# Decoder block on one core: batch 2's state ahead of the experts' first product, products on ones in TensorE's waits, and the last tile in four groups

## The reference

```python
x = _layernorm(x + ssm(x))                  # 32 complex states, linear recurrence over the 256 tokens
x = _layernorm(x + int8_expert(x, w, dw))   # per batch: smooth-quant linear, silu(gate) * up, smooth-quant linear
x = _layernorm(x + moe(x))                  # 8 experts of width 176, top 2 of 8, all experts computed densely
...
def moe(h):
    combine = top-2 softmax shares of h @ router_w.T
    for e in range(8):
        gate, up = split(h @ gate_up[e].T)
        out += combine[:, e] * ((silu(gate) * up) @ down[e].T)
```

## Time and profile before

| | |
|---|---|
| median of 3 runs | 182.44 us (182.42 to 182.51) |
| profiled execution, its own time | 181.19 us |
| its span, first to last instruction | 179.4 us |
| busy: PE, DVE, ACT, POOL | 153.3, 122.2, 88.9, 51.0 us |
| mean granted TensorE clock | 0.931 of full speed |

### The profile page before, as it was taken

The page is one execution under the profiler, slowest core; times in us unless marked ns, Lnnn a source line. Parts: engine busy times, 40 slices in busy tenths (PEclk is TensorE's granted clock), DMA queues, the critical chain, the costliest instruction groups (busy, mean ns, idle before and its releaser), DMA issues. The chain is left out here.

```text
span 179.4 us, 3021 instructions
## 1 busy us (share of the span) xinstructions
PE 153.3 (85%) x1020; PEld 141.9 (79%) x1020; DVE 122.2 (68%) x439; ACT 88.9 (50%) x211; POOL 51.0 (28%) x107
## 2 busy tenths in 40 slices
PE   7971294574969989999999999999999999999990
PEld 7850272343859979899999789999999998999980
DVE  4886777767479849668886787489567467453632
ACT  7301878663534187683224878544565523253330
POOL 5713994867901031300016211001223002100011
PEclk9999579555599999999999999999999999999999
DMA  4999930000000000000000000000000000000000
GB/s 123 290 391 394 352 120 5 0 0 0 0 2 0 5 0 0 0 4 0 0 0 33 2 27 2 4 0 0 31 4 29 0 2 4 29 29 4 0 29 29
DMA packets 6463, 8.72 MB, mean 49 GB/s; under 512 B 560, under 2 KB 6192, under 8 KB 6192
## 3 DMA queue, kind: packets, MB, share of 16 engines
q1 hardware_dynamic: 6448, 8.53, 13.8%
HBM read 7.48 MB, written 1.05 MB: 48 GB/s over the span
## 5 line engine op out<-in xcount | busy, mean ns | idle before, releaser
L284 PE MATMUL ps_gu<-gu_hi,x_hi 128*128 128x352 f32 (+1 forms) x128 | 44.7, 350 | 1.6 <-DVE hid L1487 1.6
L285 PE MATMUL ps_gu<-gu_lo,x_hi 128*128 128x352 f32 (+1 forms) x128 | 41.7, 326 | 0.0
L1487 DVE SCALAR_TENSOR_TENSOR hid<-sil,combine,ps_gu 128x176 f32<-128x176 f32 x64 | 24.1, 390 | 17.3 <-ACT sil L712 16.8
L712 ACT ACTIVATE sil<-ps_gu 128x176 f32<-128x176 f32 x64 | 19.7, 318 | 32.1 <-PE ps_gu L289 31.8
L289 PE MATMUL ps_gu<-gu_hi,x_lo 128*128 128x352 f32 (+1 forms) x128 | 31.5, 327 | 0.0
L284 PEld LDWEIGHTS ps_gu<-gu_hi,x_hi 128*128 128x128 f32 x128 | 24.5, 191 | 2.2 <-issue 1.9
L264 PE MATMUL ps_out<-dp_hi,hid_hi 128*128 128x256 f32 x88 | 25.1, 285 | 0.0
L285 PEld LDWEIGHTS ps_gu<-gu_lo,x_hi 128*128 128x128 f32 x128 | 24.5, 191 | 0.1
L265 PE MATMUL ps_out<-dp_lo,hid_hi 128*128 128x256 f32 x88 | 24.4, 278 | 0.0
L266 PE MATMUL ps_out<-dp_hi,hid_lo 128*128 128x256 f32 x88 | 24.4, 277 | 0.0
L289 PEld LDWEIGHTS ps_gu<-gu_hi,x_lo 128*128 128x128 f32 x128 | 22.5, 190 | 0.5 <-DVE x_lo L1440 0.5
(11 more groups left out here) (252 smaller groups left out, 289.6 us busy)
## 6 DMA issues: line engine op xcount, KB each, us to landing
gu_raw<-in_guT SPq DMA_DIRECT2D x1, 2824.0 KB, 11.6
dp_raw<-in_dpT SPq DMA_DIRECT2D x1, 1408.0 KB, 15.3
u_feat<-in_xT SPq DMA_DIRECT2D x4, 256.0 KB, 4.7
w_feat<-in_wT SPq DMA_DIRECT2D x4, 256.0 KB, 9.4
out<-u_feat SPq DMA_DIRECT2D x8, 128.0 KB, 1.7
dw_feat<-in_dwT SPq DMA_DIRECT2D x4, 128.0 KB, 7.2
c_raw<-in_c SPq DMA_DIRECT2D x2, 128.0 KB, 3.6
bt<-in_bT SPq DMA_DIRECT2D x1, 128.0 KB, 2.2
```

The source lines that it names most:

```text
L284: pe.matmul(dst, x2_hi[:, b % 2, c, tok], gu_hi[:, c, col], start=(c == 0), stop=False)
L285: pe.matmul(dst, x2_hi[:, b % 2, c, tok], gu_lo[:, c, col], start=False, stop=False)
L712: act.activation(sil[:, bank_of(b, k)], ps_gu[:, bank_of(b, k), E:E + H], ACT.Silu).then_inc(sil_ready, 1)
L1487: dve.scalar_tensor_tensor(hid[:, t, e * H:(e + 1) * H], sil[:, n], combine[:, t, e:e + 1], ps_gu[:, n, E + H:E + GU], ALU.mult, ALU.mult) ...
```

## The change

Four things change, and the calls of all engines are put in a new order around them.

1. `ps_state` of batch 2 becomes bank 0 of `ps_gu`, the bank of the first slot. `state_in(2)` comes behind `expert_in(0)`, `state_out(2, *)` and DVE's, POOL's and ACT's parts of batch 2's state also come ahead of `gate_up(0, 0)`, which now waits for `x1_ready` of batch 2. Batch 1's `state_out` and DVE's scan of batch 1 move ahead of batch 0's statistics and transposes, too.
2. `keep_busy` gets a bank as an argument and is called at 13 places with 87 products in all instead of 2 places with 18, the last one ahead of `gate_up(0, 0)`.
3. `down` is cut into `down_first`, which waits only for the high half of the group, and `down_second`, which waits for the low one. The products are the same.
4. The last tile's third group is cut into two (`LAST_GROUPS`): one chunk, then two.

```diff
+LAST_GROUPS = [(0, 4), (4, 8), (8, 9), (9, HC)]
...
-        ps_state = [ps_s[:], ps_gu[:, 0], ps_s[:], ps_s[:]]
+        ps_state = [ps_s[:], ps_gu[:, 0], ps_gu[:, 0], ps_s[:]]
...
-                    pe.wait_ge(x1_ready, halves(1))
+                    pe.wait_ge(x1_ready, halves(2))
...
+            def down_first(b, t, g):
+                lo, hi = groups(b, t)[g]
+                pe.wait_ge(hid_hi_ready, count_of(b, t, g))
...
                 for c in range(lo, hi):
-                    last = split_matmul(ps_out[:, 0:D], hid_hi[:, c], hid_lo[:, c], dp_hi[:, c], dp_lo[:, c],
-                                        c == 0, c == HC - 1)
-                if g == NG - 1:
+                    pe.matmul(ps_out[:, 0:D], hid_hi[:, c], dp_hi[:, c], start=(c == 0), stop=False)
+                    pe.matmul(ps_out[:, 0:D], hid_hi[:, c], dp_lo[:, c], start=False, stop=False)
+
+            def down_second(b, t, g):
+                lo, hi = groups(b, t)[g]
+                pe.wait_ge(hid_lo_ready, count_of(b, t, g))
+                for c in range(lo, hi):
+                    last = pe.matmul(ps_out[:, 0:D], hid_lo[:, c], dp_hi[:, c], start=False, stop=(c == HC - 1))
+                if hi == HC:
                     last.then_inc(moe_done, 1)
...
-                if b > 1:
+                if b == 2:
+
+                    pe.wait_ge(x1_ready, halves(1))
+                if b == 3:
 
                     pe.wait_ge(rows_ready, b)
...
-                if b == 1:
-
-                    pe.wait_ge(rows_ready, 1)
+                if b in (1, 2):
+
+                    pe.wait_ge(rows_ready, b)
                 transpose_blocks(ps_x[b], tokens[:, b], x1T_done)
...
-            def keep_busy(n):
+            def keep_busy(bank, n):
                 for _ in range(n):
-                    pe.matmul(ps_gu[:, 2, 0:P], ones[:], ones[:], start=True, stop=True)
+                    pe.matmul(bank[:, 0:P], ones[:], ones[:], start=True, stop=True)
...
+            keep_busy(ps_tr, 2)
             expert_in(0)
+            state_in(2)
             x1_transpose(1)
+            keep_busy(ps_tr, 15)
             as2_transpose(0)
             dws2_transpose(0)
+            keep_busy(ps_gu[:, 1], 2)
+            state_out(2, 0)
             scale2_broadcast(0)
+            dq_transpose(0)
             aq_transpose(0)
-            dq_transpose(0)
+            keep_busy(ps_gu[:, 1], 2)
             expert_out(0)
+            state_out(2, 1)
             xs_transpose(1)
             ws_transpose(1)
+            keep_busy(ps_gu[:, 1], 16)
             x2_transpose(0)
             xq_transpose(1)
+            keep_busy(ps_gu[:, 1], 5)
             gate_up(0, 0)
...
+            hid_transpose(3, 1, 3)
+            down_second(3, 1, 1)
+            down_first(3, 1, 2)
+            down_second(3, 1, 2)
+            down_first(3, 1, 3)
+            down_second(3, 1, 3)
```

More of the change, by code:

```diff
@@ L52, with groups, experts_to, count_of @@
 SLOT_OF = {te: k for k, te in enumerate(SLOT_ORDER)}
-ALL = [(t, g) for t in range(TT) for g in range(NG)]
-def count_of(b, group):
-    return b * len(ALL) + ALL.index(group) + 1
+def groups(b, t):
+    return LAST_GROUPS if (b, t) == (B - 1, TT - 1) else GROUPS
+def experts_to(chunk):
+    return -(-chunk * P // H)
+def count_of(b, t, g):
+    return (b * TT + t) * NG + g + 1
 def halves(b):
@@ L478, in _ @@
             state_out_s_first(1)
+            keep_busy(ps_gu[:, 2], 6)
+            state_out(1, 0)
             x1_transpose(0)
+            state_out(1, 1)
+            keep_busy(ps_tr, 7)
             xs_transpose(0)
@@ L504, in _ @@
             expert_in(1)
+            x1_transpose(2)
             gate_up(0, 3)
-            state_in(2)
             gate_up(0, 4)
             gate_up(0, 5)
-            gate_up(0, 6)
             hid_transpose(0, 0, 0)
             as2_transpose(1)
-            state_out(2, 0)
-            state_out(2, 1)
             dws2_transpose(1)
+            gate_up(0, 6)
             gate_up(0, 7)
@@ L517, in _ @@
             scale2_broadcast(1)
-            gate_up(0, 9)
-            hid_transpose(0, 0, 1)
             aq_transpose(1)
             dq_transpose(1)
-            x1_transpose(2)
+            gate_up(0, 9)
             expert_out(1)
@@ L525, in _ @@
             gate_up(0, 11)
-            down(0, 0, 0)
+            xs_transpose(2)
+            gate_up(0, 12)
+            hid_transpose(0, 0, 1)
             ws_transpose(2)
-            gate_up(0, 12)
-            xs_transpose(2)
+            down_first(0, 0, 0)
+            down_second(0, 0, 0)
+            hid_transpose(0, 0, 2)
             gate_up(0, 13)
             gate_up(0, 14)
-            hid_transpose(0, 0, 2)
             x2_transpose(1)
+            gate_up(0, 15)
             xq_transpose(2)
-            gate_up(0, 15)
-            down(0, 0, 1)
+            down_first(0, 0, 1)
             scale_broadcast(2)
-            wq_transpose(2)
             hid_transpose(0, 1, 0)
@@ L541, in _ @@
             gate_up(1, 1)
-            down(0, 0, 2)
+            down_second(0, 0, 1)
+            hid_transpose(0, 1, 1)
+            wq_transpose(2)
+            down_first(0, 0, 2)
+            down_second(0, 0, 2)
+            expert_in(2)
+            down_first(0, 1, 0)
             gate_up(1, 2)
-            expert_in(2)
-            hid_transpose(0, 1, 1)
-            down(0, 1, 0)
             gate_up(1, 3)
             state_in(3)
+            down_second(0, 1, 0)
+            hid_transpose(0, 1, 2)
+            down_first(0, 1, 1)
+            down_second(0, 1, 1)
             gate_up(1, 4)
-            hid_transpose(0, 1, 2)
             gate_up(1, 5)
-            down(0, 1, 1)
-            down(0, 1, 2)
             state_out(3, 0)
@@ L571, in _ @@
             gate_up(1, 12)
+            down_first(1, 0, 0)
             ws_transpose(3)
             xs_transpose(3)
+            down_second(1, 0, 0)
             gate_up(1, 13)
-            hid_transpose(1, 0, 2)
-            down(1, 0, 0)
             gate_up(1, 14)
             xq_transpose(3)
+            hid_transpose(1, 0, 2)
             x2_transpose(2)
@@ L581, in _ @@
             gate_up(1, 15)
-            down(1, 0, 1)
+            down_first(1, 0, 1)
+            down_second(1, 0, 1)
+            down_first(1, 0, 2)
             scale_broadcast(3)
@@ L585, in _ @@
             gate_up(2, 0)
+            down_second(1, 0, 2)
+            expert_in(3)
             gate_up(2, 1)
-            down(1, 0, 2)
             gate_up(2, 2)
-            expert_in(3)
+            down_first(1, 1, 0)
             hid_transpose(1, 1, 1)
-            down(1, 1, 0)
+            down_second(1, 1, 0)
             gate_up(2, 3)
@@ L594, in _ @@
             hid_transpose(1, 1, 2)
+            down_first(1, 1, 1)
+            down_second(1, 1, 1)
             gate_up(2, 5)
-            down(1, 1, 1)
             gate_up(2, 6)
@@ L599, in _ @@
             dws2_transpose(3)
-            down(1, 1, 2)
+            down_first(1, 1, 2)
             gate_up(2, 7)
+            down_second(1, 1, 2)
+            hid_transpose(2, 0, 0)
+            scale2_broadcast(3)
             gate_up(2, 8)
-            hid_transpose(2, 0, 0)
             aq_transpose(3)
@@ L859, in _ @@
             smooth_w(1)
+            x1_norm(2, 0)
+            x1_norm(2, 1)
+            quant_x(1, 0)
             x2_norm(0, 1)
-            quant_x(1, 0)
             quant_x(1, 1)
@@ L1663, in _ @@
             route_shares(2)
-            moe_add(1, 0)
-            gate_scale(3)
             hidden(2, 0)
+            hidden(2, 1)
+            expert_act(3)
+            hidden(2, 2)
             hid_lo_sub(1, 1, 1)
-            hidden(2, 1)
-            hidden(2, 2)
-            up_scale(3)
-            expert_act(3)
             act_ratio(3)
```

380 lines of the change are left out of this document (193 added, 187 removed).

## The result

| | before | after |
|---|---|---|
| median of 4 runs | 182.43 us (182.27 to 182.51) | 175.97 us (175.34 to 176.17) |
| profiled execution, its span | 181.19, 179.4 us | 176.10, 174.3 us |
| PE busy, mean granted clock | 153.3 us, 0.931 | 162.3 us, 0.999 |

The account below looks back on a forecast made before the run. The end was taken as the slots' start plus PE's work behind it, some 3 us of waits and a 4.6 us tail. 4.55 + 0.25 - 0.7 = 4.1 us off the median 182.44 gave 178.3 us, range 176.6 to 180.8.

Parts of the forecast that it names:

- the chain by hand: Batch 0's steps up to the fourth slot, followed at full clock: first slot 1.4 us late, fourth slot 0.25 us early.
- slower rival: Ahead of the first slot, products on ones run at half clock and delay the chain: 184.9 us, chance 0.07.
- I apply the difference to the median: Last step of the sum: 4.1 us, reckoned on the profiled execution of 181.19 us, taken off the median: 182.44 - 4.1 = 178.3 us.
- the 1.25 us: Amount by which the median of the kernel before stood above its profiled execution of 181.19 us.
- at most the 0.5 us: In the full stretch, cutting `down` can remove at most the 0.5 us that PE waited for `hid_lo`.
- 0.8 us of small waits ... I leave them: PE's small waits behind the first slot, 0.8 us, may go or be replaced; left out of the sum.
- 4.55 - 0.7: Full stretch: 4.55 us off for batch 2's state, transposes and their wait, less a new 0.7 us wait.
- The new wait for `as2`: `as2_transpose(1)`, behind slot 5, at 56.2 us on PE with its operand ready at 56.9: 0.7 us added.
- 0.25 were forecast: Ahead of the stretch: the fourth slot comes at 52.85 instead of 53.10 us, 0.25 us early.
- The rival in which the small waits go: Head's fillers cost less at `xs` (0.9), no new wait (0.7), small waits go (0.5): 176.2 us, chance 0.14.
- no change: PE's freed time all turns into waits behind 54 us: within 0.2% (0.36 us), chance 0.03.
- the shorter list meets DVE: Behind 54 us, batch 1's and 2's expert chains have less time, so waits of 1 to 3 us: around 180.3 us, chance 0.16.

Follow-up runs that it names:

- the head's 15: The changed kernel without the 15 products on ones behind `state_in(1)`, the other 72 kept: 175.53 us, ratio 0.9653.
- the earlier transfer: The changed kernel with the experts' weights' transfer issued ahead of batch 2's and 3's inputs: 175.74 us; also without the 15 products behind `state_in(1)`: 174.36 us.
- the execution of 183.3 us: The profiled execution of the kernel before, run again unchanged: 183.3 us; median of those 12 runs 181.93 us.
- the last five products: The changed kernel without the five products on ones directly ahead of the first slot: 176.01 us, ratio 0.9660.

## Why the prediction was right, and where it was wrong

**Right: the picture, and the chain by hand.** The end is the start of the slots, plus PE's work, plus a few waits, plus 4.6 us. `expert_in(0)` was put at 27.3 and came at 27.37, `expert_act(0)` at 30.74 and 30.96, `expert_out(0)` at 37.6 and 37.63, the first slot at 46.7 and 46.64, the second at 48.7 and 48.62, the fourth at 52.85 and 53.08. The stretch is the same within 0.2 us in all profiled executions of one order (121.6 to 121.8 before, 116.5 to 116.6 after, where the cut is in), and putting the state back costs its work and more.

That the absolute times fit so well is partly luck. `xs_transpose(0)` was put at 22.1 by the products at the head and DVE's chain behind them, and came at 22.13, but what held it was the experts' weights: they landed at 18.85 us, 1.14 later than in the execution shown before (17.71), and it stands 3.28 behind. In five other executions of the same head it came between 21.35 and 22.75. The intervals behind it are the reckoning's own merit: 5.2 us to `expert_in(0)` were forecast, 5.24 measured.

The full clock was an assumption of the chain, and what it is worth was in no term of its own: 3.6 us in the changed kernel. The slower rival rested on its failing, with a chance of 0.07; the clock held. The Trainium skill (TensorE: Matmul & The Clock Gate, Part 1) says that activity releases the throttle; the pair with and without the products agrees, 0.999 against 0.942 mean clock and 176.1 against 179.4 us. By the same page's Part 2, matmuls stay in program order, so a product on ones in no wait delays what follows: the head's 15 did, `x1_transpose(0)` by 1.68 us. No effect on the end was shown for it in the changed kernel, where the landing holds `xs` anyway; with the earlier transfer it was 1.4 us.

**Wrong, first: "I apply the difference to the median", the last step of the sum.** In the profiles the time went down by 181.19 - 176.10 = 5.09 us, in the medians by 6.46. These 1.37 us are more than half of the miss of 2.33. The execution shown before lay at the low end of its kernel's (181.03 to 183.65 us over all runs, 182.1 in the median), the one after near its median. Its mean clock of 0.931 was reached in 4 of the 103 other executions of that kernel whose clock is on record, at 181.1 to 181.4 us; 70 had 0.924 or less, and 182.3 us in the median. It also had the earliest landing of the experts' weights seen in that order, and the execution shown after a late one.

What made the execution of 183.3 us longer lies all ahead of the fourth slot: 1.09 us from weights that land later, at `xs`, and 0.92 between `xs` and the fourth slot. The 0.92 is clock, all of it: 0.63 in `state_out(1, 0)` and 0.29 in the second slot, with no new wait beside them (the copy of `down`'s weights came 1.08 us later, but so did `xs`). The changed order keeps its clock, and its DVE doesn't wait for batch 1's weights ahead of `xs`. For the clock experiments agree: products alone took 2.1 us off the median. For the landing nothing is shown beyond the profiles, and no execution at the median was profiled, so how the 1.37 us divide is open. Of the 1.37, 0.2 to 0.6 may be where four executions happened to fall: in the other groups the median of before was 181.9 to 182.3, not 182.43. The text had the 1.25 us in hand and should have asked which of its terms were larger in a median execution.

**Wrong, second: "at most the 0.5 us" for the cut of `down`, and "0.8 us of small waits ... I leave them".** The stretch lost 5.08 us where the sum had 4.55 - 0.7 = 3.85. The new wait for `as2` was 0.4, not 0.7 (57.11), and the small waits went. (Ahead of the stretch 0.25 were forecast and 0.02 came.) The cut is worth 2.3 us in the new order, shown by the kernel that takes it back, and 0 in the old one. So the 0.5 read from the earlier trace rows held as a bound for the old order, in which the low halves come nearly in time; in the new one they come later than the high ones are wanted. PE's waits showed 0.7 of the 2.3 when it was taken away. The rival in which the small waits go, with 0.14, stood at 176.2 us, near the 175.97 measured. That is in part luck: its 0.5 for the small waits came, but of its 0.7 for `as2` only 0.3, its 0.9 for the head's fillers not in these profiles, and it had nothing for the 1.37 us.

**Without effect, as said:** the four groups (0 predicted, 0 measured) and the last five products. The rivals "no change" and "the shorter list meets DVE" did not occur: PE's idle time in the stretch fell from 1.6 to 0.9 us. With the state back in the new order it did meet DVE, with 1.1 us for `hidden` in the stretch.

## What to carry to other kernels

Before a difference between two profiles is put on a median, find in the head of the profile what varies from run to run (transfers that an in-order engine waits for, the moment at which the clock rises) and ask whether the change removes the sensitivity. Idle stretches of TensorE in a chain that returns to it can cost more than their idle time; products on ones in them gave 2 to 4 us of 180 here; fifteen that lay in no wait cost 1.4 us as soon as nothing else held the chain. And a landmark that comes when it was forecast may be held there by something else: look at what released it. Price a finer wait together with the order that it permits: alone it can be worth nothing, taken out of the new order 2 us.
